# One operand of the half step's VectorE work in PSUM: a graph attention step whose gathers run on GpSimd

## The chip, the cores and the metric

The kernel runs on one core of one Trainium2 chip. The metric is the device time of one execution in microseconds, median over the runs. Times below are microseconds (us) unless marked ns. PE is TensorE, DVE is VectorE, ACT is ScalarE, POOL is GpSimd, SP is SyncE; L770 is line 770 of the kernel before.

## The reference

A block over 4 images of 64 x 64 pixels with 128 channels: an involution (a convolution whose 3 x 3 weights are made from the pixel), added to its input; then a mixture of four experts whose gate is a graph attention over the 16384 tokens and 524288 edges (these name nodes up to 32768; targets past the last token are dropped, sources past it read the last).

```python
def _forward(x, edge_index, W_gat, att_src, att_dst, b_gat, ln_gamma, ln_beta, W1, b1, W2, b2):
    h = (x_flat @ W_gat).reshape(M, HEADS, NUM_EXPERTS)
    src, dst = ...                                   # the edges, and a loop at each node
    a_src = (h * att_src).sum(-1)
    a_dst = (h * att_dst).sum(-1)
    e = leaky_relu(a_src[src] + a_dst[dst], negative_slope=0.2)
    e_max = segment_max(e, dst)
    ee = exp(e - e_max[dst])
    denom = segment_sum(ee, dst)
    alpha = ee / (denom[dst] + 1e-16)
    agg = segment_sum(h[src] * alpha[:, :, None], dst) + b_gat
    scores = layernorm(agg).reshape(M, HEADS, NUM_EXPERTS).mean(1)
    topk_s, topk_i = top_k(scores, 2)
    w = softmax(topk_s)
    for ei in range(NUM_EXPERTS):
        out = out + gate(w, topk_i, ei) * (gelu(x @ W1[ei] + b1[ei]) @ W2[ei] + b2[ei])
x = conv(ln(x)) + x ; x = x + _forward(ln(x), ...)
```

## The kernel before

Each engine has a program of its own, written out in order; semaphores are the only ties between them. First comes the convolution over 32 chunks of four image rows. Then the edges' keys (target node and source node in one integer) are sorted in two lists, by bitonic compares on DVE (`compare`, L1656 to L1663) with transposes on PE and copies back on ACT (`exchange`, `take_exchange`). PE and ACT compute the experts in between, chunk by chunk (`experts`, `expert_copies`): 14 chunks before the first list's exchanges, 10 after them (entry 13 of `EXPERT_CHUNKS`), and the last 8 among the second list's. PE puts four rows of a chunk into PSUM banks 4 to 7, and ACT copies each to `y_new`.

Then the first list's edges are worked through in **half steps** of 64 edges on each of 128 partitions. There are 16 in this run, numbered n = 2k + u here, 0 to 15; step k has halves u = 0 and 1. For each:

- DVE's `new_sources`, two steps ahead, takes the source nodes from the keys.
- POOL's `half` issues one gather for the targets' scores (`adw`, NEAR = 16 neighbouring nodes of 4 heads, L770) and 64 row gathers (`rows_of`, one `indirect_dma_start` of 128 rows each, L770, into `rows_g`, four buffers). At u = 0 it then does `store_fix(k - 3)` (L774) and `fetch_fix(k - 2)`, which carry a node's sums over from one step to the next. POOL's program is in this order and waits where a semaphore isn't there.
- DVE's `half` sorts a part of the second list (`SORTED_BY`), then does `chain_runs(k - 1)` at u = 0 or `mend(k - 2)` at u = 1 (its last line, L2004, lets `store_fix` go), then `edge_scans`. That begins with `nearby`: a one-hot `hot` (L1879) and for each of 4 heads a product (L1884, the pick) and a sum over 16 words (L1886). It then waits for the gathered rows (L1911), makes the scores and running maxima, waits for ACT's exponentials, weights the rows (L1940) and adds up along each partition with a scan (L1948) over 4 heads x 5 parts x 64 edges.
- ACT's `half` takes its exchanges and expert chunks, the small exponentials, and then `edge_exponentials`, whose last copy puts the sums in order for the store to HBM.

After the last half step come a short loop over the second list's edges (`trip`), the gathers of each node's sums (`agg`), the gate, and the mixing of the experts' outputs.

Of the kernel before, what the change touches and what calls it, by code (L numbers as in the profile page):

```python
# [90 lines left out]
def metaformer_block(nc, x, Wr, br, gamma, beta, mean, var, Ws, bs, Wi, bi,  # L91
# [3 lines left out]
    with ctx:  # L95
# [6 lines left out]
        def sem(name):  # L102
# [151 lines left out]
        drop = sb("drop", [P, HEADS, T], F32, edge)  # L254
        keep = sb("keep", [P, HEADS, PARTS - 1, T], F32, edge)
        sums_x = sb("sums_x", [P, HEADS, PARTS - 1, T], F32, edge)
        new = sb("new", [P, HEADS, PARTS - 1, T], F32, edge)
        high = sb("high", [P, 1 + HEADS * T], F32, edge)
# [21 lines left out]

        chain_n = new[0:HEADS].rearrange("p h j t -> p (h j t)")[:, 0:P * (PARTS - 1)].rearrange(
            "p (c j) -> p c j", j=PARTS - 1)
        hot = keep.rearrange("p h j t -> p (h j t)")[:, 0:T * NEAR].rearrange("p (t n) -> p t n", n=NEAR)
        picked = new.rearrange("p h j t -> p (h j t)")[:, 0:T * NEAR].rearrange("p (t n) -> p t n", n=NEAR)
        samples = late[:, 0:P]
# [21 lines left out]
        def sems(names):  # L307
# [33 lines left out]
            sems(f"{n}0 {n}1") for n in ("dch_in", "dch_used", "keys_in", "state_out", "tnT_back", "y_out"))  # L341
        (scored, weighed, state_ready, tails_stored, tails_loaded, chain_scored, chain_weighed,
         summed, chain_ready, chain_stored, cprev_loaded, fix_placed, fix_got, fix_scored,
         fix_weighed, fix_ready, fix_stored, agg_cleared) = sems(
            "scored weighed state_ready tails_stored tails_loaded chain_scored chain_weighed "
            "summed chain_ready chain_stored cprev_loaded fix_placed fix_got fix_scored "
# [554 lines left out]
        def _(pe):  # L901
# [91 lines left out]
            def experts(g, u, turn, q):  # L993
                pe.wait_ge(tnT_back[u], 16 * (turn + 1))
                for e in range(EXPERTS):
                    for a in (0, 1):
                        n = 2 * e + a
                        if some(8 * g + n - 3):
                            pe.wait_ge(hid_ready, 8 * g + n - 3)
                        pe.matmul(bank[n % 4][:, :], w1[:, e, a * P:(a + 1) * P], tnT_in[:, u],  # L1000
                                  start=TR, stop=TR).then_inc(hid_psum, 1)
                pe.wait_ge(hid_ready, 8 * g + 8)
                for r in range(ROWS):
                    if some(g):
                        pe.wait_ge(y_taken, ROWS * (g - 1) + r + 1)
                    po = bank[4 + r]
                    pe.matmul(po[:, :], ones[:, :], b2_rows[:, :], start=TR, stop=FA)
                    for e in range(EXPERTS):
                        for a in (0, 1):
                            last = pe.matmul(po[:, e * C:(e + 1) * C],  # L1010
                                             hid[u][:, 2 * e + a, r * P:(r + 1) * P], w2[:, e, a],
                                             start=FA, stop=e == EXPERTS - 1 and a == 1)
                    last.then_inc(y_psum, 1)
# [21 lines left out]
        def _(act):  # L1035
# [141 lines left out]
            def expert_copies(g, v, turn, q):  # L1177
                for n in range(8):
                    act.wait_ge(hid_psum, 8 * g + n + 1)
                    if n == 0 and some(g - 1):  # L1180
                        act.wait_ge(y_psum, ROWS * (g - 1))
                    act.activation(hid[v][:, n], bank[n % 4][:, :], ACT.Gelu,  # L1182
                                   bias=b1c[:, n // 2, n % 2:n % 2 + 1]).then_inc(hid_ready, 1)

                act.dma_start(tnT_in[:, v], tnT_d[ds(g + 2, 1)].squeeze(0)).then_inc(tnT_back[v], 16)
                if some(turn):
                    act.wait_ge(y_out[v], 32 * turn)
                for r in range(ROWS):
                    act.wait_ge(y_psum, ROWS * g + r + 1)
                    act.activation(y_new[:, v, r], bank[4 + r][:, :], ACT.Copy).then_inc(y_taken, 1)  # L1190
# [8 lines left out]
            def fix_exponentials(k):  # L1199
                act.wait_ge(fix_scored, k + 1)  # L1200
                act.activation(fixe[:, :, :], fixe[:, :, :], ACT.Exp).then_inc(fix_weighed, 1)

            def edge_exponentials(k, u):
                act.wait_ge(scored, 2 * k + u + 1)
                act.activation(keep[:, :, :, :], over(drop[:, :, :], PARTS - 1, 2), ACT.Exp)  # L1205
                if u == 1:
                    act.activation(carry[:, 1], carry[:, 1], ACT.Exp)
                act.activation(new[:, :, 0], score[:, :, :], ACT.Exp).then_inc(weighed, 1)
                act.activation(state_parts[:, u, :, 0], high[:, 1:].rearrange("p (h t) -> p h t", t=T), ACT.Copy)
                act.wait_ge(summed, 2 * k + u + 1)  # L1210
                act.activation(state_parts[:, u, :, 1:], sums_x[:, :, :, :], ACT.Copy).then_inc(state_ready, 1)

# [11 lines left out]
            def half(k, u, j, pair, b):  # L1224
# [49 lines left out]
        def _(dve):  # L1274
# [614 lines left out]
            def edge_scans(k, u, j, pair, b):  # L1889
# [46 lines left out]
                if some(k):  # L1936
                    dve.wait_ge(state_out[u], 16 * k)
                dve.tensor_tensor(drop[:, :, :], drop[:, :, :], reset[:, :, :], ALU.add).then_inc(scored, 1)  # L1938
                dve.wait_ge(weighed, 2 * k + u + 1)
                dve.tensor_tensor(new[:, :, 1:], rows_g[:, w, :, 0:HE].rearrange("p t (h e) -> p h e t", e=EXPERTS),  # L1940
                                  over(new[:, :, 0], EXPERTS, 2), ALU.mult)
                if u == 1:
                    dve.tensor_tensor(carried[:, :, :], sums_x[:, :, :, T - 1], over(carry[:, 1], PARTS - 1, 2),
                                      ALU.mult)
# [244 lines left out]
```

## Time and profile before

| | |
|---|---|
| median of 3 runs | 2920.72 us (2920.6 to 2924.26) |
| span of the profiled execution (its first to its last instruction; it has no other time of its own) | 2918.8 us |
| busy DVE / POOL / PE / ACT | 74% / 45% / 35% / 27% of the span |
| half steps (first L1879 to last L1948) | 1353.9 to 2595.4 us |
| row gathers | 1024, from 1100.0 to 2581.4 us |

The profile is one execution as the hardware recorded it. A row of a timeline has a start, a duration, the engine, the line, what it writes and reads, and in brackets how long the engine stood idle before it and what ended that. "issue" is idle time that no semaphore explains.

### The profile page before, as it was taken

To read this page: it belongs to the slowest core of one execution; us is meant where nothing else is said; L and a number is where in the kernel's file an instruction comes from. 1 tells how busy PE (TensorE), PEld (TensorE's weight loads), DVE (VectorE), ACT (ScalarE), POOL (GpSimd) and SP (SyncE) were. 2 spreads that over 40 slices of the span, in tenths; PEclk is the share of its full clock that TensorE was granted. 3 is DMA by queue.
4 is the path that set the end of the run, shared out by engine and by line. 5 is a ranking of instruction groups with operands and counts; after the bars stand their busy time and mean duration, and the time that the engine had idled before them with its cause. 6 is when DMAs were issued, how large, how long until landed. Compare 5 with 4: busy or idle time off the path is not lost.

```text
span 2918.8 us, 22141 instructions
## 1 busy us (share of the span) xinstructions
PE 1017.2 (35%) x4867; PEld 685.7 (23%) x4867; DVE 2168.2 (74%) x4017; ACT 785.0 (27%) x1576; POOL 1315.3 (45%) x1234
## 2 busy tenths in 40 slices
PE   6777776599811110499333333310000000000000
PEld 3544454366511100266222222210000000000000
DVE  5999989999699974998888898856334313822888
ACT  3555544244411100144322222311000000000344
POOL 0000000000000007777777777778777777835750
PEclk8777666799955555699666666655555555555555
DMA  2222325992100011133231313142212113333676
GB/s 57 72 72 73 78 64 194 384 112 77 71 0 0 0 18 28 30 81 91 44 41 37 42 37 42 37 53 27 19 19 23 19 12 21 46 33 86 182 230 223
DMA packets 259502, 202.29 MB, mean 69 GB/s; under 512 B 101592, under 2 KB 207445, under 8 KB 258902
## 3 DMA queue, kind: packets, MB, share of 16 engines
q1 hardware_dynamic: 189766, 114.21, 17.5%
q0 software_dynamic: 46336, 44.61, 9.1%
q10 hardware_dynamic: 23314, 42.60, 4.6%
q14 instruction: 66, 0.54, 0.1%
q8 instruction: 20, 0.33, 0.0%
HBM read 94.51 MB, written 107.07 MB: 69 GB/s over the span
## 4 chain that ended last, share of the span: by engine, by line
POOL 40%; DVE 15%; issue 15%; PE 14%; DVEq 9%; DMA 3%; ACT 2%; ACTq 0%; POOLq 0%; SPq 0%
POOL sb_rows_g L770 38%; PE bank L1010 4%; DVE sb_xi L1656 3%; PE bank L1000 3%; DVEq L1672 2%; PE bank L926 2%; DVE sb_inv L1361 2%; DVEq L1392 1%; DVE sb_xi L1663 1%; DVEq L1382 1%; DVE sb_y_new L2146 1%; DVE sb_stats L1334 1%; PE bank L917 1%; POOL sb_agg L770 1%; DVEq L1387 1%
## 5 line engine op out<-in xcount | busy, mean ns | idle before, releaser
L770 POOL DMA_INDIRECT sb_rows_g<-scr_node,sb_srcs x1024 | 1107.3, 1081 | 312.1 <-issue 312.1
L1663 DVE TENSOR_TENSOR sb_xi<-sb_xi 128x512 f32<-128x512 f32 (+2 forms) x852 | 427.1, 568 | 46.8 <-ACT sb_xi L1159 33.0
L989 PE MATMUL bank<-sb_ident,sb_xi 128*128 128x128 f32 x448 | 99.5, 410 | 533.6 <-DVE sb_xi L1663 280.1
L770 POOL DMA_INDIRECT sb_hid_y<-scr_level,sb_row_at x8 | 9.3, 1163 | 597.2 <-DVE sb_row_at L1420 595.0
L1656 DVE TENSOR_TENSOR sb_xi<-sb_xi 128x1024 f32<-128x1024 f32 (+2 forms) x258 | 243.5, 944 | 28.2 <-ACT sb_xi L1164 9.5
L1000 PE MATMUL bank<-sb_tnT_in,sb_w 128*128 128x512 f32 x512 | 243.8, 630 | 58.0 <-DVE sb_sinks L1768 33.5
L1010 PE MATMUL bank<-sb_w,sb_hid_y 128*128 128x128 f32 x2048 | 262.6, 282 | 0.0
L1657 DVE TENSOR_TENSOR sb_xi<-sb_xi 128x1024 f32<-128x1024 f32 (+2 forms) x258 | 245.9, 953 | 0.0
L1010 PEld LDWEIGHTS bank<-sb_w,sb_hid_y 128*128 128x128 f32 x2048 | 238.2, 192 | 29.0 <-issue 29.0
L1182 ACT ACTIVATE sb_hid_y<-bank,sb_b1c 128x512 f32<-128x512 f32 x256 | 163.6, 691 | 239.2 <-PE bank L1000 237.5
L765 POOL DMA_DIRECT2D scr_adst_at_starts<-sb_zeros x1 | 1.1, 1057 | 487.3 <-DMA sb_xi<-in_L_ffn_edge_index 487.3
L1031 PE MATMUL bank<-sb_ident,sb_sinks 128*128 128x128 f32 x1 | 0.5, 477 | 616.7 <-DVE sb_sinks L2031 616.7
L989 PEld LDWEIGHTS bank<-sb_ident,sb_xi 128*128 128x128 f32 x448 | 85.7, 216 | 545.5 <-DVE sb_xi L1663 286.2
L1911 DVE TENSOR_TENSOR sb_score<-sb_rows_g,sb_df 128x256 f32<-128x256 f32 x16 | 10.9, 683 | 254.9 <-DMA sb_rows_g<-scr_node,sb_srcs 254.1
L1355 DVE TENSOR_TENSOR sb_prod<-sb_xi,sb_wv 128x1152 f32<-128x1152 f32 x128 | 172.7, 1349 | 23.2 <-ACT sb_xi L1065 18.5
L1205 ACT ACTIVATE sb_keep<-sb_drop 128x1280 f32<-128x1280 f32 x16 | 20.3, 1269 | 614.9 <-DVE sb_drop L1938 614.8
L1361 DVE TENSOR_REDUCE sb_inv<-sb_prod 128x128 f32<-128x1152 f32 x128 | 172.0, 1344 | 5.9 <-issue 1.2
L770 POOL DMA_INDIRECT sb_agg<-scr_state,sb_posi x128 | 132.1, 1032 | 44.2 <-issue 38.7
L1031 PEld LDWEIGHTS bank<-sb_ident,sb_sinks 128*128 128x128 f32 x1 | 0.2, 183 | 616.9 <-DVE sb_sinks L2031 616.9
L1000 PEld LDWEIGHTS bank<-sb_tnT_in,sb_w 128*128 128x128 f32 x512 | 99.7, 202 | 181.4 <-issue 146.0
L1190 ACT ACTIVATE sb_y_new<-bank 128x512 f32<-128x512 f32 x128 | 76.4, 597 | 243.6 <-PE bank L1010 243.6
L926 PE MATMUL bank<-sb_wi,sb_xnT 128*128 128x128 f32 x768 | 140.4, 328 | 0.0
(337 smaller groups left out, 2175.8 us busy)
## 6 DMA issues: line engine op xcount, KB each, us to landing
scr_expert_out<-sb_y_new ACTq DMA_DIRECT2D x64, 512.0 KB, 3.8
sb_y_in<-scr_expert_out SPq DMA_DIRECT2D x32, 1024.0 KB, 6.8
scr_state<-sb_zeros POOLq DMA_DIRECT2D x6, 4096.0 KB, 55.9
sb_rows_g<-scr_node,sb_srcs POOLq DMA_INDIRECT x1024
scr_state<-sb_state SPq DMA_DIRECT2D x16, 768.0 KB, 7.0
scr_tnT<-sb_tnT SPq DMA_DIRECT2D x34, 256.0 KB, 2.0
sb_tnT_in<-scr_tnT ACTq DMA_DIRECT2D x34, 256.0 KB
sb_xa<-in_x SPq DMA_DIRECT2D x64, 128.0 KB, 2.5
```

What stands on the lines that cost most here:

```text
L770: pool.indirect_dma_start(to, None, table, bass.IndirectOffsetOnAxis(ap=index, axis=0), **kw).then_inc(s, 16)
L926: last = pe.matmul(po[:, j * C:(j + 1) * C], xnT[:, u, r, 2 * j:2 * j + P], wi[:, :], start=FA, stop=j == 2)
L989: last = pe.transpose(bank[b][:, m * P:(m + 1) * P], src[:, (4 * b + m) * P:(4 * b + m + 1) * P], ident[:, :])
L1000: pe.matmul(bank[n % 4][:, :], w1[:, e, a * P:(a + 1) * P], tnT_in[:, u], start=TR, stop=TR).then_inc(hid_psum, 1)
L1010: last = pe.matmul(po[:, e * C:(e + 1) * C], hid[u][:, 2 * e + a, r * P:(r + 1) * P], w2[:, e, a], start=FA, stop=e == EXPERTS - 1 and a == 1)
L1182: act.activation(hid[v][:, n], bank[n % 4][:, :], ACT.Gelu, bias=b1c[:, n // 2, n % 2:n % 2 + 1]).then_inc(hid_ready, 1)
L1190: act.activation(y_new[:, v, r], bank[4 + r][:, :], ACT.Copy).then_inc(y_taken, 1)
L1355: return dve.tensor_tensor(to.rearrange("p (g f k) -> p g f k", g=GROUPS, k=KK), patch.rearrange("p (g f k) -> p g f k", g=GROUPS, k=KK), ...
L1361: dve.tensor_reduce(inv[:, r], prod[:, r % 2 * TAPS:(r % 2 + 1) * TAPS].rearrange("p (o k) -> p o k", k=KK), AX.X, ALU.add)
L1656: dve.tensor_tensor(vb[:, :, 0], va[:, :, 0], va[:, :, 1], ALU.min)
L1657: last = dve.tensor_tensor(vb[:, :, 1], va[:, :, 0], va[:, :, 1], ALU.max)
L1663: last = dve.tensor_tensor(vb[:, :, d, :, c], va[:, :, d, :, 0], va[:, :, d, :, 1], ALU.min if c == d else ALU.max)
```

## The change

In `nearby`, in the weighting and in the scan, one of the two operands comes from PSUM bank 7. The experts give that bank up and take banks 4, 5, 6 in turn (`y_bank`, `y_free`). ACT has a new step, `place_around`, ahead of `edge_exponentials`: it copies the target scores (heads first, so that a head's 16 words lie side by side) and the constants 0 to 15 into the bank, and DVE's `nearby` waits for that (`around_placed`). The exponentials of `keep` and of the weights go to the bank too, `keep` once and not five times; a second copy of the weights stays in `new`. `keep`, `sums_x` and `new` have the part ahead of the head, and the scan becomes five, one for each part, over the same `keep`.

```diff
-        hot = keep.rearrange("p h j t -> p (h j t)")[:, 0:T * NEAR].rearrange("p (t n) -> p t n", n=NEAR)
+        flat_keep = bank[7][:, HEADS * T:2 * HEADS * T]
+        weights, keep = (bank[7][:, k * HEADS * T:(k + 1) * HEADS * T].rearrange("p (h t) -> p h t", t=T)
+                         for k in (0, 1))
+        around = bank[7][:, 0:WORDS].rearrange("p (h n) -> p h n", n=NEAR)
+        steps_of = bank[7][:, WORDS:WORDS + NEAR]
...
+        def y_bank(u, r):
+
+            return bank[4 + (r + u) % 3]
+
+        def y_free(g, u, r):
+
+            return ROWS * g + 1 if r == 3 else ROWS * (g - 1) + ((3, 4, 2), (2, 3, 4))[u][r]
...
-                    if some(g):
-                        pe.wait_ge(y_taken, ROWS * (g - 1) + r + 1)
-                    po = bank[4 + r]
+                    if r == 3 or some(g):
+                        pe.wait_ge(y_taken, y_free(g, u, r))
+                    po = y_bank(u, r)
...
+            def place_around(k, u, pair, w):
+                act.wait_ge(adw_in[w], 16 * (pair + 1))
+                if some(2 * k + u):
+                    act.wait_ge(summed, 2 * k + u)
+                act.activation(around, adw[:, w].rearrange("p (n h) -> p h n", h=HEADS), ACT.Copy)
+                act.activation(steps_of, nearest[:, :], ACT.Copy).then_inc(around_placed, 1)
...
-                act.activation(keep[:, :, :, :], over(drop[:, :, :], PARTS - 1, 2), ACT.Exp)
+                act.activation(keep, drop[:, :, :], ACT.Exp)
...
-                act.activation(new[:, :, 0], score[:, :, :], ACT.Exp).then_inc(weighed, 1)
+                act.activation(weights, score[:, :, :], ACT.Exp)
+                act.activation(new[:, 0], score[:, :, :], ACT.Exp).then_inc(weighed, 1)
...
+                place_around(k, u, pair, 2 * b + u)
                 edge_exponentials(k, u)
...
-                dve.tensor_tensor(hot, over(rel[:, w], NEAR, 2), over(nearest[:, :], T), ALU.is_equal)
+                dve.wait_ge(around_placed, 2 * k + u + 1)
+                dve.tensor_tensor(hot[:, :, :], over(rel[:, w], NEAR, 2), over(steps_of, T), ALU.is_equal)
...
-                    dve.tensor_tensor(picked, hot, over(adw[:, w, h:WORDS:HEADS], T), ALU.mult)
+                    dve.tensor_tensor(picked, hot[:, :, :], over(around[:, h], T), ALU.mult)
...
-                dve.tensor_tensor(new[:, :, 1:], rows_g[:, w, :, 0:HE].rearrange("p t (h e) -> p h e t", e=EXPERTS),
-                                  over(new[:, :, 0], EXPERTS, 2), ALU.mult)
+                dve.tensor_tensor(new[:, 1:], rows_g[:, w, :, 0:HE].rearrange("p t (h e) -> p e h t", e=EXPERTS),
+                                  over(weights, EXPERTS, 1), ALU.mult)
...
-                dve.tensor_tensor_scan(flat(sums_x), flat(keep), flat(new), 0.0, ALU.mult, ALU.add).then_inc(summed, 1)
+                for part in range(PARTS - 1):
+                    last = dve.tensor_tensor_scan(flat(sums_x[:, part]), flat_keep, flat(new[:, part]), 0.0,
+                                                  ALU.mult, ALU.add)
+                last.then_inc(summed, 1)
```

How it stands in DVE's order at the start of half step 0's `edge_scans`, before (`sb_keep` holds the one-hot there, `sb_new` the picked words):

```order
L1893 COPY sb_run_now<-sb_run_next 128x3
L1879 TENSOR_TENSOR sb_keep<-sb_rel,sb_nearest 128x1024
L1881 TENSOR_SCALAR sb_afar<-sb_rel 128x64 [waits adw_in0]
L1884 TENSOR_TENSOR sb_new<-sb_keep,sb_adw 128x1024
L1886 TENSOR_REDUCE sb_drop<-sb_new 128x64
```

And in the changed kernel:

```order
L1916 COPY sb_run_now<-sb_run_next 128x3
L1902 TENSOR_TENSOR sb_hot<-sb_rel,bank 128x1024 [waits around_placed]
L1904 TENSOR_SCALAR sb_afar<-sb_rel 128x64 [waits adw_in0]
L1907 TENSOR_TENSOR sb_new<-sb_hot,bank 128x1024
L1909 TENSOR_REDUCE sb_drop<-sb_new 128x64
```

The first product of the half step has a wait for ACT, and `sb_nearest` and `sb_adw` have become the bank; nothing has changed its place. At the half step's end on DVE (weighting, scan, and the first line of `new_sources`), before:

```order
L1938 TENSOR_TENSOR sb_drop<-sb_drop,sb_reset 128x256
L1940 TENSOR_TENSOR sb_new<-sb_rows_g,sb_new 128x4x256 [waits weighed]
L1948 SCALAR_TENSOR_TENSOR sb_sums_x<-sb_keep,sb_new 128x1280
L1519 TENSOR_SCALAR sb_srcs<-sb_keyb 128x64 [waits keys_in0]
L1520 TENSOR_SCALAR sb_clsi<-sb_keyb 128x65
```

And in the changed kernel:

```order
L1961 TENSOR_TENSOR sb_drop<-sb_drop,sb_reset 128x256
L1963 TENSOR_TENSOR sb_new<-sb_rows_g,bank 128x1024 [waits weighed]
L1972 SCALAR_TENSOR_TENSOR sb_sums_x<-bank,sb_new 128x256 x5
L1541 TENSOR_SCALAR sb_srcs<-sb_keyb 128x64 [waits keys_in0]
L1542 TENSOR_SCALAR sb_clsi<-sb_keyb 128x65
```

One scan of 1280 elements (the order prints a scan by this name) has become five of 256. On ACT, from the end of the ten expert chunks into half step 0, before:

```order
L1193 DMA scr_expert_out<-sb_y_new 64x4x512
L477 REGISTER_ALU
L477 COMPARE_AND_BRANCH
L1205 ACT_TABLE_LOAD [waits scored]
L1205 ACTIVATE sb_keep<-sb_drop 128x1280 [waits counted]
L1208 ACTIVATE sb_new<-sb_score 128x4x64
```

And in the changed kernel:

```order
L1205 DMA scr_expert_out<-sb_y_new 64x4x512
L489 REGISTER_ALU
L489 COMPARE_AND_BRANCH
L1219 ACTIVATE bank<-sb_adw 128x64 [waits adw_in0,counted]
L1220 ACTIVATE bank<-sb_nearest 128x16
L1224 ACT_TABLE_LOAD
L1224 ACTIVATE bank<-sb_drop 128x256 [waits scored]
L1227 ACTIVATE bank<-sb_score 128x256
L1228 ACTIVATE sb_new<-sb_score 128x256
```

The two copies into the bank stand behind all expert chunks and ahead of the half step's exponentials.

## Rows read from the trace of the kernel before

**Rows 1.** The page: the chain that ended last, by line.

```profile
POOL sb_rows_g L770 38%; PE bank L1010 4%; DVE sb_xi L1656 3%; PE bank L1000 3%; DVEq L1672 2%; PE bank L926 2%; DVE sb_inv L1361 2%; DVEq L1392 1%; DVE sb_xi L1663 1%; DVEq L1382 1%; DVE sb_y_new L2146 1%; DVE sb_stats L1334 1%; PE bank L917 1%; POOL sb_agg L770 1%; DVEq L1387 1%
```

**Rows 2.** The page's costliest groups: busy, mean ns | idle before, its releaser.

```profile
L770 POOL DMA_INDIRECT sb_rows_g<-scr_node,sb_srcs x1024 | 1107.3, 1081 | 312.1 <-issue 312.1
...
L1911 DVE TENSOR_TENSOR sb_score<-sb_rows_g,sb_df 128x256 f32<-128x256 f32 x16 | 10.9, 683 | 254.9 <-DMA sb_rows_g<-scr_node,sb_srcs 254.1
```

**Rows 3.** One line's instructions, L770: count, ns min/median/max, first and last start.

```profile
L770 POOL DMA_INDIRECT sb_rows_g<-scr_node,sb_srcs x1024: 940/944/3073, 1100.0 to 2581.4; - x171
```

**Rows 4.** Timeline of POOL in half step 1: start, duration, engine, line, operands.

```profile
1424.25 0.94 POOL L770 DMA_INDIRECT sb_rows_g<-scr_node,sb_srcs  x1 [0.30 <-issue]
...
1433.22 1.74 POOL L770 DMA_INDIRECT sb_rows_g<-scr_node,sb_srcs  x1 [0.30 <-issue]
1435.27 0.94 POOL L770 DMA_INDIRECT sb_rows_g<-scr_node,sb_srcs  x1 [0.30 <-issue]
1436.52 1.79 POOL L770 DMA_INDIRECT sb_rows_g<-scr_node,sb_srcs  x1 [0.30 <-issue]
...
1455.52 1.99 POOL L770 DMA_INDIRECT sb_rows_g<-scr_node,sb_srcs  x1 [0.30 <-issue]
1457.82 2.96 POOL L770 DMA_INDIRECT sb_rows_g<-scr_node,sb_srcs  x1 [0.31 <-issue]
```

**Rows 5.** Timeline of DVE in the same stretch.

```profile
1424.23 1.28 DVE L1657 TENSOR_TENSOR sb_xi<-sb_xi 128x1024 f32<-128x1024 f32 x1
...
1432.17 1.97 DVE L1884 TENSOR_TENSOR sb_new<-sb_keep,sb_adw 128x1024 f32<-128x1024 f32 x1
1434.21 1.22 DVE L1886 TENSOR_REDUCE sb_drop<-sb_new 128x64 f32<-128x1024 f32 x1
...
1446.75 0.69 DVE L1904 TENSOR_TENSOR_SCAN sb_df<-sb_same,sb_dch_h 128x256 f32<-128x256 f32 x1
...
1448.01 0.43 DVE L1908 TENSOR_TENSOR sb_df<-sb_df,sb_drop 128x256 f32<-128x256 f32 x1
1448.51 0.68 DVE L1911 TENSOR_TENSOR sb_score<-sb_rows_g,sb_df 128x256 f32<-128x256 f32 x1
...
1454.48 2.28 DVE L1940 TENSOR_TENSOR sb_new<-sb_rows_g,sb_new 128x1024 f32<-128x1024 f32 x1 [1.74 <-ACT sb_new L1208]
...
1457.19 2.82 DVE L1948 TENSOR_TENSOR_SCAN sb_sums_x<-sb_keep,sb_new 128x1280 f32<-128x1280 f32 x1
```

**Rows 6.** Timeline of DVE and ACT around half step 0.

```profile
1353.87 1.22 DVE L1879 TENSOR_TENSOR sb_keep<-sb_rel,sb_nearest 128x1024 f32<-128x1024 f32 x1
...
1387.72 2.29 DVE L1940 TENSOR_TENSOR sb_new<-sb_rows_g,sb_new 128x1024 f32<-128x1024 f32 x1 [12.52 <-ACT sb_new L1208]
...
1382.38 0.60 ACT L1190 ACTIVATE sb_y_new<-bank 128x512 f32<-128x512 f32 x1 [1.70 <-PE bank L1010]
1383.18 1.41 ACTq L1193 DMA_DIRECT2D scr_expert_out<-sb_y_new  x2
...
1386.11 1.27 ACT L1205 ACTIVATE sb_keep<-sb_drop 128x1280 f32<-128x1280 f32 x1
1387.29 0.40 ACT L1208 ACTIVATE sb_new<-sb_score 128x256 f32<-128x256 f32 x1
```

**Rows 7.** Timeline of DVE and POOL in half steps 5 and 7.

```profile
1732.99 0.19 DVE L2004 TENSOR_TENSOR sb_fixo<-sb_cprev,sb_fixs 128x20 f32<-128x20 f32 x1
...
1734.22 1.18 POOL L774 DMA_INDIRECT scr_state<-sb_fixo,sb_fixo_i  x1 [0.30 <-issue]
...
1911.76 0.18 DVE L2002 TENSOR_TENSOR sb_cprev<-sb_cprev,sb_fixe 128x20 f32<-128x20 f32 x1 [12.86 <-ACT sb_fixe L1201]
...
1912.10 0.18 DVE L2004 TENSOR_TENSOR sb_fixo<-sb_cprev,sb_fixs 128x20 f32<-128x20 f32 x1
...
1923.56 1.02 POOL L774 DMA_INDIRECT scr_state<-sb_fixo,sb_fixo_i  x1 [0.30 <-issue]
```

**Rows 8.** Windows, tile `rows_g`: from and to, length, busy us (count), PE clock, DMA.

```profile
1923.50:2583.00 659.50, 23.72 (x16) 486.41 (x448) 0.50 0.24 25
```

More of the change, by code:

```diff
@@ L185, in metaformer_block @@
         carry = sb("carry", [P, 3, HEADS])
-        carried = sb("carried", [P, HEADS, PARTS - 1])
+        carried = sb("carried", [P, PARTS - 1, HEADS])
         keyb = sb("keyb", [P, 2, 1 + 2 * T], I32)
@@ L254, in metaformer_block @@
         drop = sb("drop", [P, HEADS, T], F32, edge)
-        keep = sb("keep", [P, HEADS, PARTS - 1, T], F32, edge)
-        sums_x = sb("sums_x", [P, HEADS, PARTS - 1, T], F32, edge)
-        new = sb("new", [P, HEADS, PARTS - 1, T], F32, edge)
+        hot = sb("hot", [P, T, NEAR], F32, edge)
+        sums_x = sb("sums_x", [P, PARTS - 1, HEADS, T], F32, edge)
+        new = sb("new", [P, PARTS - 1, HEADS, T], F32, edge)
         high = sb("high", [P, 1 + HEADS * T], F32, edge)
@@ L279, in metaformer_block @@
         edge.close()
-        chain_n = new[0:HEADS].rearrange("p h j t -> p (h j t)")[:, 0:P * (PARTS - 1)].rearrange(
+        chain_n = new[0:HEADS].rearrange("p j h t -> p (j h t)")[:, 0:P * (PARTS - 1)].rearrange(
             "p (c j) -> p c j", j=PARTS - 1)
-        hot = keep.rearrange("p h j t -> p (h j t)")[:, 0:T * NEAR].rearrange("p (t n) -> p t n", n=NEAR)
-        picked = new.rearrange("p h j t -> p (h j t)")[:, 0:T * NEAR].rearrange("p (t n) -> p t n", n=NEAR)
+        flat_keep = bank[7][:, HEADS * T:2 * HEADS * T]
[3 more added lines that the diff above has]
+        steps_of = bank[7][:, WORDS:WORDS + NEAR]
+        picked = new.rearrange("p j h t -> p (j h t)")[:, 0:T * NEAR].rearrange("p (t n) -> p t n", n=NEAR)
         samples = late[:, 0:P]
@@ L341, in metaformer_block @@
             sems(f"{n}0 {n}1") for n in ("dch_in", "dch_used", "keys_in", "state_out", "tnT_back", "y_out"))
-        (scored, weighed, state_ready, tails_stored, tails_loaded, chain_scored, chain_weighed,
+        (around_placed, scored, weighed, state_ready, tails_stored, tails_loaded, chain_scored, chain_weighed,
          summed, chain_ready, chain_stored, cprev_loaded, fix_placed, fix_got, fix_scored,
          fix_weighed, fix_ready, fix_stored, agg_cleared) = sems(
-            "scored weighed state_ready tails_stored tails_loaded chain_scored chain_weighed "
+            "around_placed scored weighed state_ready tails_stored tails_loaded chain_scored chain_weighed "
             "summed chain_ready chain_stored cprev_loaded fix_placed fix_got fix_scored "
@@ L1189, in expert_copies @@
                     act.wait_ge(y_psum, ROWS * g + r + 1)
-                    act.activation(y_new[:, v, r], bank[4 + r][:, :], ACT.Copy).then_inc(y_taken, 1)
+                    act.activation(y_new[:, v, r], y_bank(v, r)[:, :], ACT.Copy).then_inc(y_taken, 1)
                 act.wait_ge(y_taken, ROWS * (g + 1))
@@ L1201, in fix_exponentials @@
                 act.activation(fixe[:, :, :], fixe[:, :, :], ACT.Exp).then_inc(fix_weighed, 1)
+            def place_around(k, u, pair, w):
[4 more added lines that the diff above has]
+                act.activation(steps_of, nearest[:, :], ACT.Copy).then_inc(around_placed, 1)
             def edge_exponentials(k, u):
                 act.wait_ge(scored, 2 * k + u + 1)
-                act.activation(keep[:, :, :, :], over(drop[:, :, :], PARTS - 1, 2), ACT.Exp)
+                act.activation(keep, drop[:, :, :], ACT.Exp)
                 if u == 1:
                     act.activation(carry[:, 1], carry[:, 1], ACT.Exp)
-                act.activation(new[:, :, 0], score[:, :, :], ACT.Exp).then_inc(weighed, 1)
+                act.activation(weights, score[:, :, :], ACT.Exp)
+                act.activation(new[:, 0], score[:, :, :], ACT.Exp).then_inc(weighed, 1)
                 act.activation(state_parts[:, u, :, 0], high[:, 1:].rearrange("p (h t) -> p h t", t=T), ACT.Copy)
                 act.wait_ge(summed, 2 * k + u + 1)
-                act.activation(state_parts[:, u, :, 1:], sums_x[:, :, :, :], ACT.Copy).then_inc(state_ready, 1)
+                act.activation(state_parts[:, u, :, 1:], sums_x.rearrange("p j h t -> p h j t"),
+                               ACT.Copy).then_inc(state_ready, 1)
             def exchanges(first, end):
@@ L1939, in edge_scans @@
                 dve.wait_ge(weighed, 2 * k + u + 1)
-                dve.tensor_tensor(new[:, :, 1:], rows_g[:, w, :, 0:HE].rearrange("p t (h e) -> p h e t", e=EXPERTS),
-                                  over(new[:, :, 0], EXPERTS, 2), ALU.mult)
+                dve.tensor_tensor(new[:, 1:], rows_g[:, w, :, 0:HE].rearrange("p t (h e) -> p e h t", e=EXPERTS),
+                                  over(weights, EXPERTS, 1), ALU.mult)
                 if u == 1:
-                    dve.tensor_tensor(carried[:, :, :], sums_x[:, :, :, T - 1], over(carry[:, 1], PARTS - 1, 2),
+                    dve.tensor_tensor(carried[:, :, :], sums_x[:, :, :, T - 1], over(carry[:, 1], PARTS - 1, 1),
                                       ALU.mult)
```

## The prediction

> **What bounds the kernel now.** VectorE (DVE) is the busiest engine, but a busy share says nothing of who sets the end, so I first read the chain that ended last [rows 1]. Its largest entry is line 770 on GpSimd (POOL): the row gathers, 38%. So in the stage of the half steps, 1350 to 2590 us, I asked who waits for whom [rows 2]. DVE's line 1911, which needs the 64 gathered rows of its half step, sat idle 254 us before 7 of its 16 executions; the 1024 gathers sat idle 312 us, all of it their own 0.30 us between two. POOL never waits for DVE there; DVE, when it is ahead, waits for POOL. The end is set by how long 1024 gathers take.
>
> Then I asked how long one takes. The undisturbed gather is 0.94 us (least 940, median 944 ns), but the longest took 3073 ns and the mean is 1081 [rows 2, 3]. The timelines of POOL and of DVE over one half step, laid side by side, say where the rest comes from [rows 4, 5]. The gather that starts at 1433.22 takes 1.74; DVE's pick product (line 1884) runs from 1432.17 to 1434.14, and the gather ends 0.82 us after that. The gather that begins at 1435.27, under the reduction of line 1886, takes 0.94. The gather at 1455.52 ends 0.7 to 0.8 us after line 1940, and that at 1457.82 takes 2.96 and ends 0.8 us after the scan of line 1948. So a gather that begins under one of these three lines stands still until that DVE instruction is over. All three read two tensors from SBUF; the reduction, which reads one, does no harm. One row speaks less clearly: the sort's compare at 1424.23 reads two as well, and the gather at 1424.25 takes 0.94. That gather begins within 0.02 us of the compare's start, so it may have read before the compare did.
>
> **What the stretch is worth.** The two picks shown cost 1.74 and 1.79 less 0.94 each, 0.8 on the mean, so the four of a half step 3.3 us of POOL's time; the other two lines cost 1.99 + 2.96 less 1.88 = 3.07 us. That is 6.4 us, or 102 us over 16 half steps. In every one of the changed instructions one of the two tensors now lies in PSUM. No row shows a DVE instruction with one operand in each memory; between a stretch that stays whole and none at all I take none, since the form is nearest to the reduction, with one SBUF input. The other two-input lines are left as they are.
>
> The Trainium skill (SBUF — State Buffer, Who interferes with whom) says two things here: VectorE with two SBUF inputs contends with a GpSimd instruction that reads SBUF, and with one it does not; but also that a probe saw `tensor_tensor` leave descriptor generation alone. Rows 4 and 5 speak against the second; if it held, the stretch would have another cause and could stay, as in the second rival below.
>
> **What the change does to DVE.** POOL's gain is worth something only where DVE does not stop POOL, so DVE's time comes next. Per half step:
> - Picks: the picked words were read 4 words apart (`adw[:, w, h:WORDS:HEADS]`); they now lie side by side. Lines 1879 and 1884 have the same size, 1024 elements, and take 1.22 and 1.97 [rows 5, 6]; the words' stride is what differs. That a stride costs is seen again at 256 elements: line 1911, which reads rows 20 words apart, takes 0.68, line 1908 takes 0.43 [rows 5]. Bounds for the new pick: 1.22 and 1.97. I take 1.22, so 4 x 0.75 = 3.0 us less.
> - Exponentials: ACT's 1.27 us over 1280 elements and 0.40 over 256 become three of 256, 1.20 in all: 0.5 us less in the wait before line 1940 [rows 6].
> - Scans: one of 2.82 becomes five of 256. A scan of 256 takes 0.69, so the five lie between 2.82 and 3.46: I take 0.5 more.
> - Line 1940 keeps its strided rows: 0.
>
> Together 3.0 us less per half step. Neither half of this reaches the end by itself, since DVE waits for the gathers later; at the very end, after the last gather, 0.5 less and 0.5 more cancel.
>
> The Trainium skill (VectorE: DVE Perf Modes, The TRN2 errata) gives a source in PSUM 120 fixed cycles against 58 for SBUF. For 11 instructions that would be an estimated 0.7 us per half step, and would put the end some 5 us later than my sum; no row here has this form.
>
> **What it adds: a wait at half step 0.** DVE may now start `nearby` only when ACT has copied `adw` into the bank, and ACT does that behind all it has queued. In half step 0 ACT is still copying the ten expert chunks out of PSUM: its last copy starts at 1382.38, two DMA issues end at 1384.6, and two copies smaller than those of 0.40 us follow, so the bank is ready near 1385.3. Before, DVE started line 1879 at 1353.87 and met ACT only at line 1940, where it waited 12.52 us [rows 6]. So DVE starts 31.4 us later; the wait of 12.52 shrinks to the ordinary 1.74 (half step 1) less 0.5, which is 11.3 less; picks 3.0 less; scans 0.5 more: half step 0 ends 17.6 us later. In later half steps ACT is done with its experts before DVE needs the bank, and the two copies are hidden; the closest is half step 7, where DVE waits 12.86 us for ACT anyway just ahead of line 2004 [rows 7] and the copies come right behind that; the later DMA wait for `adw` on ACT holds nothing that DVE lacks.
>
> **Where DVE then stops POOL.** POOL's `store_fix` (line 774) in half step 6 needs DVE's `mend` (line 2004), which ends 1733.18; POOL starts it at 1734.22: a cover of 1.0 us. In half step 8 it is 1912.28 against 1923.56, a cover of 11.3 [rows 7]. DVE reaches the first 17.6 - 4 x 3.0 = 5.6 us later, so POOL starts it at 1739.8, though its own gathers would have let it come at 1734.2 - 5 x 6.4 = 1702. The gain of the first five half steps turns into a wait of 38 us. From there to the second point POOL took 189.3 us; without the stretches of half steps 5, 6 and the picks of 7 (2 x 6.4 + 3.3 = 16.1) it takes 173.2: 1913.0. DVE's own time there is 1912.28 + 17.6 - 6 x 3.0 = 1911.9, and POOL follows 1.0 later: 1912.9, just under that. Before: 1923.56. Gain so far: 10.6 us.
>
> After that point DVE is ahead of POOL (the seven waits of line 1911 all lie there), and POOL sets the end alone. What its gathers lose: by the pattern 3.07 (half step 7) + 7 x 6.4 + 3.3 (half step 15) = 51 us; by the window from 1923.5 to 2583, 486.41 - 448 x 0.944 = 63.5 us of stretch of every cause [rows 8]. I take 57, half way. Sum: 10.6 + 57 = 68 us. The rest, from the last gather on, moves along unchanged. So do the experts: with three banks in turn, a chunk's fourth row waits for the copy of its first, 0.60 us long, and PE takes 2.3 us for each row between (ACT waits 1.70 for it before each copy) [rows 6].
>
> The profiled span is 2918.8, the median of the runs 2920.7, 1.9 us more around it: 2920.7 - 68 = **2853 us**.
>
> **The rivals.**
> - Picks stay at 1.97 (PSUM read no faster). Then DVE gains nothing per half step and half step 0 ends 20.6 later; POOL passes the second point at 1933.9, 10.3 late, and gains 57 after it: 47 less, 2874. For it: no row has the form. Against: the stride is gone in either memory.
> - The stretch isn't tied to the second SBUF input, but to the length of a DVE instruction of this kind. The picks, shorter by 0.74, would stretch 0.1 each instead of 0.8, the other two lines as before: 2.9 of 6.4 goes. After the second point 57 x 2.9 / 6.4 = 26 us are gained, and 1913.0 moves to 1739.8 + 189.3 - 16.1 x 2.9 / 6.4 = 1921.8, 2 us gained: 2893. For it: the stretches grow with the instruction's length. Against: the reduction is 1.22 long and harmless. The gather beside the sort's compare speaks for it too.
> - The late start doesn't reach POOL, and all 102 us count: 2819. Against it: a cover of 1.0 us at half step 6.
> - Slower: reading PSUM beside SBUF is slow on DVE. DVE would hold POOL at half step 8. The sum is zero when DVE is 67 us late there (57 + 10.3); 20.6 is the wait of half step 0, so 47 us over 7 half steps, 6.7 each: picks of 1.97 + 1.7 = 3.7 us. At 4.3 us a pick it would be 9.3 more per half step, and 2939.
>
> **How the numbers follow.** The forecast (2843 to 2866 with its own bounds: 51 to 63.5 of stretch, scans 2.82 to 3.46, 0.1 us more for a pick) 0.64; picks not faster 0.13; stretch tied to length 0.10; all 102 us 0.05; slow PSUM, slower 0.04; and 0.04 for a gain that something unseen takes back to nothing. A measurement of this kernel tells about 0.2% from no change. So faster 0.92, same 0.04, slower 0.04. The range, 2838 to 2896, takes in the first three cases and leaves 0.13 outside.
>
> **What would show it.** In the changed trace: gathers under lines 1907, 1963 and 1972 at 0.94; picks at 1.2 to 1.3 us; a DVE wait of about 31 us for ACT line 1220 in half step 0; a POOL wait of some 38 us at line 774 of half step 6, for DVE's `mend`, and next to none in half step 8; the last gather near 2514 instead of 2581. If gathers still take 1.8 us beside the picks, the reading of rows 4 and 5 was wrong; if picks stay near 2 us, that of the stride; if POOL doesn't wait at half step 6, my time for DVE.

## The result, and the profile after

The changed kernel took 2840.61 us (median of 4, 2834.66 to 2846.96) against 2920.66 us for the kernel before (median of 4, 2912.6 to 2924.26): ratio 0.9721, interval 0.9689 to 0.9754, 80 us less. The forecast was 2853, 12 us above.

The page of the changed kernel: its span, the chain that ended last, and the groups that answer to [rows 1, 2].

```profile
span 2832.8 us, 22266 instructions
...
DVE 28%; PE 21%; POOL 18%; DVEq 14%; issue 10%; ACT 5%; DMA 3%; ACTq 1%; SPq 0%; POOLq 0%
...
L782 POOL DMA_INDIRECT sb_rows_g<-scr_node,sb_srcs x1024 | 1001.4, 978 | 312.1 <-issue 311.7
...
L1934 DVE TENSOR_TENSOR sb_score<-sb_rows_g,sb_df 128x256 f32<-128x256 f32 x16 | 10.9, 682 | 210.8 <-DMA sb_rows_g<-scr_node,sb_srcs 210.0
```

The mean gather fell from 1081 to 978 ns; the pause of 0.30 us between two is as it was. The row gathers were 38% of the chain [rows 1]; on this page they are 16% (all of POOL 18%), and DVE is 28%. The timeline of POOL under the picks, the weighting and the scans of half step 1 answers to [rows 4]:

```profile
1438.79 0.94 POOL L782 DMA_INDIRECT sb_rows_g<-scr_node,sb_srcs  x1 [0.31 <-issue]
1440.04 0.94 POOL L782 DMA_INDIRECT sb_rows_g<-scr_node,sb_srcs  x1 [0.30 <-issue]
1441.29 0.94 POOL L782 DMA_INDIRECT sb_rows_g<-scr_node,sb_srcs  x1 [0.30 <-issue]
...
1452.68 1.22 POOL L782 DMA_INDIRECT sb_rows_g<-scr_node,sb_srcs  x1 [0.30 <-issue]
...
1459.20 0.94 POOL L782 DMA_INDIRECT sb_rows_g<-scr_node,sb_srcs  x1 [0.30 <-issue]
1460.45 0.94 POOL L782 DMA_INDIRECT sb_rows_g<-scr_node,sb_srcs  x1 [0.30 <-issue]
1461.69 0.94 POOL L782 DMA_INDIRECT sb_rows_g<-scr_node,sb_srcs  x1 [0.30 <-issue]
```

And DVE's in the same stretch, which answers to [rows 5]:

```profile
1438.98 1.22 DVE L1907 TENSOR_TENSOR sb_new<-sb_hot,bank 128x1024 f32<-128x1024 f32 x1
1440.27 1.22 DVE L1909 TENSOR_REDUCE sb_drop<-sb_new 128x64 f32<-128x1024 f32 x1
...
1452.46 0.68 DVE L1934 TENSOR_TENSOR sb_score<-sb_rows_g,sb_df 128x256 f32<-128x256 f32 x1
...
1457.92 2.29 DVE L1963 TENSOR_TENSOR sb_new<-sb_rows_g,bank 128x1024 f32<-128x1024 f32 x1 [1.19 <-ACT sb_new L1228]
...
1460.64 3.01 DVE L1972 TENSOR_TENSOR_SCAN sb_sums_x<-bank,sb_new 128x256 f32<-128x256 f32 x5
```

Gathers that begin well inside the picks, the weighting or the scans now take 0.94: the one at 1459.20 begins 1.28 us into the weighting and ends before it. Beside a product that still reads two tensors from SBUF (L1934 at 1452.46) one of 1.22 is left.

For the whole program I put what each of the 1024 row gathers took above 0.944 us down to the DVE line that it overlapped longest (the sums are mine, over the rows of each trace; the last two columns are experiments told of below):

| stretch of row gathers under, us | before | changed | everything in SBUF | words alone in PSUM |
|---|---|---|---|---|
| one-hot, picks and their reductions | 59.4 | 0.2 | 17.0 | 0.2 |
| weighting | 17.5 | 0.0 | 15.3 | 14.5 |
| scans | 26.1 | 0.0 | 3.9 | 3.9 |
| all other lines | 37.7 | 34.6 | 34.5 | 32.7 |

Under the changed lines the gathers lost 103 us before and lose 0.2 now; the prediction counted 102. Not all of that reaches the end. The timelines around half step 0, then of POOL in half steps 6 and 8, answer to [rows 6, 7]:

```profile
1374.42 0.28 ACT L1219 ACTIVATE bank<-sb_adw 128x64 f32<-128x64 f32 x1 [1.85 <-issue]
1374.64 0.17 ACT L1220 ACTIVATE bank<-sb_nearest 128x16 f32<-128x16 f32 x1
...
1344.59 0.17 DVE L1916 COPY sb_run_now<-sb_run_next 128x3 f32<-128x3 f32 x1
1374.84 1.22 DVE L1902 TENSOR_TENSOR sb_hot<-sb_rel,bank 128x1024 f32<-128x1024 f32 x1 [30.08 <-ACT bank L1220]
...
1726.05 0.18 DVE L2030 TENSOR_TENSOR sb_fixo<-sb_cprev,sb_fixs 128x20 f32<-128x20 f32 x1
1727.11 1.02 POOL L786 DMA_INDIRECT scr_state<-sb_fixo,sb_fixo_i  x1 [40.59 <-DVE sb_fixo L2030]
...
1896.44 0.18 DVE L2030 TENSOR_TENSOR sb_fixo<-sb_cprev,sb_fixs 128x20 f32<-128x20 f32 x1
1899.38 1.02 POOL L786 DMA_INDIRECT scr_state<-sb_fixo,sb_fixo_i  x1 [0.30 <-issue]
```

DVE waits 30 us for two small copies that stand behind ACT's ten expert chunks. Some 350 us after that, POOL has stood still for 40.6 us before `store_fix` of half step 6, waiting for DVE's `mend`. In half step 8 it comes 2.8 us after `mend` and doesn't wait.

The two profiled executions differ by 86.0 us of span: 9.2 ahead of half step 0, 72.7 from there to the last row gather, and 4.1 behind it. So stage times below are counted from half step 0, from DVE's copy to `run_now` (at 1353.8 before, 1344.6 here), to the end: 1565.0 us before, and 1488.2 and 1489.4 in two profiles of the changed kernel.

### The profile page after: what moved, and what is told of

It is laid out like the page before. It is cut to its first block, busy times and chain, and to the rows that moved or that the text cites. A ratio compares the mean times of both kernels' runs of the same rounds, so it can differ in the third digit from the quotient of the medians.

```text
span 2832.8 us, 22266 instructions
## 1 busy us (share of the span) xinstructions
PE 1002.3 (35%) x4867; PEld 675.7 (24%) x4867; DVE 2124.0 (75%) x4081; ACT 780.2 (28%) x1624; POOL 1202.6 (42%) x1234
## 4 chain that ended last, share of the span: by engine, by line
DVE 28%; PE 21%; POOL 18%; DVEq 14%; issue 10%; ACT 5%; DMA 3%; ACTq 1%; SPq 0%; POOLq 0%
POOL sb_rows_g L782 16%; PE bank L1022 7%; DVE sb_xi L1678 7%; PE bank L1012 6%; DVEq L1694 5%; DVE sb_xi L1685 3%; DVE sb_inv L1383 2%; PE bank L938 2%; DVE sb_hid_y L1518 2%; DVEq L1414 2%; PE bank L1001 2%; DVEq L1404 2%; DVE sb_y_new L2172 1%; PE bank L1019 1%; DVE sb_new L1907 1%
## 5 line engine op out<-in xcount | busy, mean ns | idle before, releaser
L782 POOL DMA_INDIRECT sb_rows_g<-scr_node,sb_srcs x1024 | 1001.4, 978 | 312.1 <-issue 311.7
L1012 PE MATMUL bank<-sb_tnT_in,sb_w 128*128 128x512 f32 x512 | 238.5, 618 | 57.7 <-DVE sb_sinks L1790 33.5
L1377 DVE TENSOR_TENSOR sb_prod<-sb_xi,sb_wv 128x1152 f32<-128x1152 f32 x128 | 172.7, 1350 | 20.0 <-ACT sb_xi L1077 15.3
L1934 DVE TENSOR_TENSOR sb_score<-sb_rows_g,sb_df 128x256 f32<-128x256 f32 x16 | 10.9, 682 | 210.8 <-DMA sb_rows_g<-scr_node,sb_srcs 210.0
L1224 ACT ACTIVATE bank<-sb_drop 128x256 f32<-128x256 f32 x16 | 6.2, 388 | 538.6 <-DVE sb_drop L1961 538.6
```

The costliest lines, as they stand in the source:

```text
L782: pool.indirect_dma_start(to, None, table, bass.IndirectOffsetOnAxis(ap=index, axis=0), **kw).then_inc(s, 16)
L1377: return dve.tensor_tensor(to.rearrange("p (g f k) -> p g f k", g=GROUPS, k=KK), patch.rearrange("p (g f k) -> p g f k", g=GROUPS, k=KK), ...
```

## The experiments

Two theories stood against each other. **A**: a gather that begins under a DVE instruction with two SBUF inputs stands still until that ends; one operand in PSUM sets it free. **B**: the stretch belongs to long instructions of this kind, and it went because picks and scans became short. With either, the late start at half step 0 may or may not pass to POOL.

**Everything in SBUF.** The changed kernel with its layout and order, but what lay in the bank lies in a tile in SBUF.

```diff
+        half_work = sb("half_work", [P, 2 * HEADS * T], F32, edge)
...
-        flat_keep = bank[7][:, HEADS * T:2 * HEADS * T]
+        flat_keep = half_work[:, HEADS * T:2 * HEADS * T]
...
-        around = bank[7][:, 0:WORDS].rearrange("p (h n) -> p h n", n=NEAR)
+        around = half_work[:, 0:WORDS].rearrange("p (h n) -> p h n", n=NEAR)
```

> The changed kernel with its four tiles (words, constants, weights, keep) in SBUF instead of the bank: the new layout, the five scans and ACT's step stay, only PSUM goes. Theory A (a gather that begins under a DVE instruction with two SBUF inputs stands still until that instruction ends): picks are 1.22 us and side by side now, so a gather falls into step with them and loses about 0.1 us per pick; it loses about 1.05 us under the weighting (2.28 us) and some 1 us under the five scans: 2.4 us per half step, 19 us after the second point where DVE can hold POOL and a few before it, so 20 to 24 us more than the changed kernel, about 2862 us. Theory B (only the length of a DVE instruction counts, wherever its operands lie): nothing changes, 2841 us, within 5.

Measured: 2863.02 us against 2922.32 for the kernel before on the same chip (0.9787, 0.9729 to 0.9845); from half step 0 to the end 24.8 us more than the changed kernel, as A has it. Its gathers on the page, 35 ns longer than in the changed kernel:

```profile
L783 POOL DMA_INDIRECT sb_rows_g<-scr_node,sb_srcs x1024 | 1037.3, 1013 | 312.0 <-issue 311.7
```

POOL and DVE on the timeline of its half step 1:

```profile
1442.45 0.94 POOL L783 DMA_INDIRECT sb_rows_g<-scr_node,sb_srcs  x1 [0.30 <-issue]
1443.69 1.05 POOL L783 DMA_INDIRECT sb_rows_g<-scr_node,sb_srcs  x1 [0.30 <-issue]
...
1459.29 2.68 POOL L783 DMA_INDIRECT sb_rows_g<-scr_node,sb_srcs  x1 [0.30 <-issue]
1462.27 1.40 POOL L783 DMA_INDIRECT sb_rows_g<-scr_node,sb_srcs  x1 [0.30 <-issue]
...
1442.70 1.23 DVE L1908 TENSOR_TENSOR sb_new<-sb_hot,sb_half_work 128x1024 f32<-128x1024 f32 x1
1445.29 1.23 DVE L1908 TENSOR_TENSOR sb_new<-sb_hot,sb_half_work 128x1024 f32<-128x1024 f32 x1
...
1458.93 2.29 DVE L1964 TENSOR_TENSOR sb_new<-sb_rows_g,sb_half_work 128x1024 f32<-128x1024 f32 x1 [1.19 <-ACT sb_new L1229]
...
1461.64 3.05 DVE L1973 TENSOR_TENSOR_SCAN sb_sums_x<-sb_half_work,sb_new 128x256 f32<-128x256 f32 x5
```

The weighting is the clean pair: 2.29 us long in both kernels. With one input in the bank, the gather at 1459.20 took 0.94; with both in SBUF, that at 1459.29 takes 2.68 and ends 0.75 us after the weighting; the next, under the scans, takes 1.40. So with all of them: 14 gathers that begin more than 0.1 us into the weighting take 1.75 to 2.69 here and end 0.75 to 0.76 us after it, and 19 such gathers of the changed kernel take 0.94 to 0.95. Only the memory of one operand differs, so B falls as the whole cause, and A is shown.

The picks show something else. With their words side by side they stretch a gather by no more than 0.1 us even from SBUF (1443.69). The gather at 1442.45 began 0.25 us ahead of a pick and ran through it at 0.94, so one that is under way isn't stopped; the next begins near the pick's end. A pick and its reduction take 2.59 us (1442.70 to 1445.29), and two gathers with their pauses 0.94 + 0.30 + 1.05 + 0.30 = 2.59: the gathers have fallen in step with DVE. In the table above, the layout alone takes 42 of the picks' 59 us and 22 of the scans' 26, in all 67 of the 103; the bank takes the other 36.

**Words alone in PSUM.** The picks' operands stay in the bank; `weights` and `keep` go to SBUF.

```diff
...
-        weights, keep = (bank[7][:, k * HEADS * T:(k + 1) * HEADS * T].rearrange("p (h t) -> p h t", t=T)
+        weights, keep = (half_work[:, k * HEADS * T:(k + 1) * HEADS * T].rearrange("p (h t) -> p h t", t=T)
```

> Half of the change: words and constants in the bank, weights and keep in SBUF. Theory A: the picks leave the gathers alone (0.94), the weighting with two SBUF inputs costs the gather under it about 1.05 us again, and the five scans (0.66 us each, end to end) about 1 us together: 2 us per half step, 16 us after the second point, so 2857 us. Theory B: 2841 us.

Measured: 2855.04 us (0.9744, 0.9686 to 0.9803, against the same runs of before), 11.1 us more than the changed kernel from half step 0 on. That is 5 less than A's figure, since five short scans stretch the gathers by 0.24 us per half step (3.9 / 16), not by 1. The weighting's 0.9 (14.5 / 16) is as expected, and the picks' column is clean again. The same instruction does harm or not, by where its second input lies.

**Words 4 apart in the bank.** Only the order of the copied words changes.

```diff
-        around = bank[7][:, 0:WORDS].rearrange("p (h n) -> p h n", n=NEAR)
+        around = bank[7][:, 0:WORDS].rearrange("p (n h) -> p h n", h=HEADS)
```

> The changed kernel, but the words stay in their old order in the bank, so that a pick reads them 4 apart from PSUM. Theory A: the gathers beside the picks stay at 0.94 us however long a pick is. If the stride costs in PSUM what it did in SBUF (1.97 us a pick), DVE is 3.0 us later per half step and holds POOL at half step 8 some 16 us longer: 2857 us; if it costs nothing there, 2841. Theory B: with picks of 1.97 us the gathers under them go back to 1.74 to 1.80, 3.3 us per half step, 27 us after the second point and the 16 before it: about 2884 us.

The lines of the picks, one source line each: of this kernel, of the changed one, and of the one with everything in SBUF (least, median and greatest ns):

```profile
L1907 DVE TENSOR_TENSOR sb_new<-sb_hot,bank x64: 1220/1221/1223, 1399.9 to 2500.4; 128x1024 f32<-128x1024 f32 x64
```

```profile
L1907 DVE TENSOR_TENSOR sb_new<-sb_hot,bank x64: 1220/1221/1223, 1376.2 to 2476.9; 128x1024 f32<-128x1024 f32 x64
```

```profile
L1908 DVE TENSOR_TENSOR sb_new<-sb_hot,sb_half_work x64: 1224/1225/1226, 1377.2 to 2500.3; 128x1024 f32<-128x1024 f32 x64
```

The stride that made 1.97 us of 1.22 in SBUF costs nothing in the bank. So this run gave no slow pick, and could not set A apart from B as it was meant to: 2838.14 us (0.9687, 0.9631 to 0.9744), 0.6 us from the changed kernel in the stage.

**The wait alone.** The kernel before, and in it only the wait: ACT copies the words to a tile `aside` in SBUF that nobody reads, and `nearby` waits for it.

```diff
+                act.activation(aside[:, 0:WORDS], adw[:, w], ACT.Copy)
+                act.activation(aside[:, WORDS:], nearest[:, :], ACT.Copy).then_inc(around_placed, 1)
...
+                dve.wait_ge(around_placed, 2 * k + u + 1)
                 dve.tensor_tensor(hot, over(rel[:, w], NEAR, 2), over(nearest[:, :], T), ALU.is_equal)
```

> The kernel before, with the new wait alone: ACT copies the words and constants to a tile in SBUF that nobody reads, and DVE's nearby waits for that; the operands stay where they were. My theory: DVE starts half step 0 31 us later and ends it 20 us later, POOL's cover of 1.0 us at half step 6 is gone and it waits about 19 us there, and since nothing became faster all of it stays: about 1584 us from half step 0 to the end against 1565, and some 19 us slower than before. Rival (the late start is absorbed by DVE's slack): the time of before.

Measured: 2936.11 us against 2919.06 (1.0057, 1.0033 to 1.0081), 17 us more, and 17.3 more from half step 0 on. The timeline of POOL in half step 6:

```profile
1759.47 1.33 POOL L775 DMA_INDIRECT scr_state<-sb_fixo,sb_fixo_i  x1 [21.14 <-DVE sb_fixo L2012]
```

The late start passes to POOL almost whole: `mend` comes 18.8 us later than before, against a cover of 1.0.

**Words placed early.** ACT makes half step 0's two copies ahead of the ten expert chunks. This kernel was run twice, the second time beside the changed kernel as it is.

```diff
                         act.wait_ge(search_over, 1)
+                        place_around(0, 0, 0, 0)
                     over_experts(act, expert_copies, n)
...
-                place_around(k, u, pair, 2 * b + u)
+                if some(2 * k + u):
+                    place_around(k, u, pair, 2 * b + u)
```

> The changed kernel with ACT's copy of half step 0's words put ahead of the ten expert chunks, so that the wait at half step 0 goes (30.1 us in the profile of the changed kernel), but the old wait for the exponentials (12.5 us before) comes back. My theory: DVE ends half step 0 about 16 us earlier, reaches the two places where it holds POOL 16 us earlier, POOL's wait at half step 6 shrinks from 40.6 to about 25 us, and all of it reaches the end: 2825 us. Rival: POOL, not DVE, sets the second point by its own pace from somewhere else, or the late start is absorbed: 2841 us.

> The kernel with half step 0's words copied early, once more. In its profile the stretch from half step 0 to the end was 20 us shorter than in the changed kernel, and POOL's wait at half step 6 was 21 us and not 41, as my theory has it; but its times were those of the changed kernel, with a convolution of 540 us in the profiled run. If that was the draw of the convolution: some 15 to 20 us below the changed kernel's times on this chip. If early words cost the same 20 us somewhere ahead of half step 0: no difference again, and a long convolution in the profile again.

> The changed kernel once more, beside the others on one chip. The convolution ahead of the half steps took between 513 and 540 us in the profiles so far, with PE's granted clock going up and down between its two levels in another pattern each time, so a single time says little within 10 us. From the start of half step 0 to the end the profiles should agree: 1488 us here as in the first profile of the changed kernel, whatever the convolution took.

Measured: 2838.57 us the first time (0.9697 of before, 0.9636 to 0.9758) and 2825.79 the second (0.9676, 0.9644 to 0.9707), beside 2838.81 for the changed kernel (0.9741, 0.9702 to 0.9781). The first time shows no gain over the changed kernel and misses the 2825 that was expected; the second shows 13 us. The stage says it plainly both times: 20 us less from half step 0 to the end than the changed kernel (1468.1 and 1469.8 against 1488.2 and 1489.4), and POOL in half step 6 waits half as long; the timeline of the second:

```profile
1729.45 1.02 POOL L786 DMA_INDIRECT scr_state<-sb_fixo,sb_fixo_i  x1 [19.96 <-DVE sb_fixo L2032]
```

What hid this the first time lies ahead of half step 0, which began at 1371.2 us in its profile and at 1344.6 in the changed kernel's. That is no price of the early words: the kernel with words 4 apart, which has none, began it at 1367.9. It is the convolution: from its last reciprocal (L1367 in the changed kernel) to half step 0 all ten profiles take 829.0 to 830.3 us.

**POOL's step moved behind.** Words placed early, and in steps 3 to 5 `store_fix` and `fetch_fix` come at u = 1 and not at u = 0, so that POOL has issued one more half step of gathers before it needs `mend`.

```diff
-                if u == 0 and (not isinstance(k, int) or k > 2):
-                    store_fix(k - 3)
+                tail_or_first = (isinstance(j, int) and j < 0) or (isinstance(k, int) and k == 2)
+                if u == (0 if tail_or_first else 1):
+                    if not isinstance(k, int) or k > 2:
+                        store_fix(k - 3)
...
```

> Early words, and POOL's store_fix and fetch_fix of steps 3 to 5 one half step later in its order (behind the gathers of half u = 1), so that DVE's mend is long over when POOL comes to them. My theory, that these two waits are where DVE still holds POOL: POOL waits nowhere between half step 0 and the last gather, the last 21 us of waiting go, and from half step 0 to the end it takes about 1447 us (1468 with early words alone, 1488 changed, 1565 before). Rival: DVE holds POOL elsewhere, or the later fetch stops DVE's mend so that gathers wait for sources: no gain over early words alone.

Measured: 2809.72 us (2801.68 to 2829.8) against 2919.06 for before (0.9636, 0.9594 to 0.9678) and 2838.81 for the changed kernel; it beats both. From half step 0 to the end 1451.7 us, 36.5 less than the changed kernel and 16 to 18 less than with early words alone, where 1447 was expected. From half step 0 to the last row gather POOL waits for no other engine for longer than its usual 0.3 us. POOL's waits by what it waited for (total, times, longest), of the changed kernel and of this one:

```profile
POOL scr_state L786 <- DVE sb_fixo L2030: 50.5, 2, 40.6
```

```profile
POOL scr_state L786 <- DVE sb_fixo L2034: 10.0, 1, 10.0
```

The wait of 40.6 is gone; that of 10, behind the last row gather, was there before (9.9).

## Why the prediction was right

**The stretch.** It goes whole, as taken: 103 us of it lay under the changed lines, 102 were counted, and 0.2 is left. The sum agrees better than its terms: picks with their one-hot had 59 where 53 were counted, weighting and scans 44 where 49 were. And the prediction put all of it down to PSUM, while 67 of the 103 go by the new layout alone, with everything in SBUF; the step from two SBUF inputs to one is worth the other 36, and 24.8 us of the stage.

That the stretch hangs on the second SBUF input, and not on length, rested in the prediction on one reduction, and its row can't carry that. The gather of 1435.27 begins 0.16 us before that reduction's end (1435.43), and with the 0.75 to 0.8 us that a stopped gather takes after the end it would have had about 0.94 either way. So this step was right by luck as far as the row goes. The weighting at one length with its operand in either memory shows it, and the changed kernel has gathers that begin early in a reduction and take 0.94 (23 that begin more than 0.4 us before its end take 0.94 to 0.95):

```profile
1385.54 0.94 POOL L782 DMA_INDIRECT sb_rows_g<-scr_node,sb_srcs  x1 [0.30 <-issue]
...
1385.30 1.22 DVE L1909 TENSOR_REDUCE sb_drop<-sb_new 128x64 f32<-128x1024 f32 x1
```

The row that spoke less clearly, the gather of 0.94 beside the sort's compare, is a near thing and no exception. Before the change 66 gathers begin within 0.05 us behind a compare of L1657. Of these 63 take 0.94, and the compare then takes 1.27 to 1.29; three take 2.0, and the compare 1.22, as here:

```profile
1643.79 1.22 DVE L1657 TENSOR_TENSOR sb_xi<-sb_xi 128x1024 f32<-128x1024 f32 x1
...
1643.82 2.00 POOL L770 DMA_INDIRECT sb_rows_g<-scr_node,sb_srcs  x1 [0.30 <-issue]
```

That fits the prediction's guess, that one of the two may read first; a gather that begins 0.25 us ahead isn't stopped (1442.45 with everything in SBUF).

The Trainium skill (SBUF — State Buffer, Who interferes with whom) has VectorE contend with GpSimd's reads when both its inputs come from SBUF, and not with one; the weighting agrees, 2.68 against 0.94 us. The probe that the Trainium skill reports there, in which `tensor_tensor` did not stall a DMA, isn't borne out by these gathers (2.68 us); they also read their indices from SBUF (`sb_srcs`), and which part of a gather stands still no run shows.

**DVE.** Picks 1.22 as taken. The five scans 3.01 us where 3.3 was taken (between 2.82 and 3.46), so DVE gains a little more than 3.0 per half step: from the end of half step 0 (the last line of `new_sources`) to the `mend` of half step 5 it takes 325.0 us after 338.4, 13.4 less where 12.0 was predicted. The weighting kept its 2.28, and the wait before it fell to 1.19 (1.24 predicted).

The Trainium skill (VectorE: DVE Perf Modes, The TRN2 errata) would add an estimated 0.7 us per half step for sources in PSUM; these rows don't show it: the pick takes 1.221 us from the bank and 1.225 from SBUF, the weighting 2.28 from either.

**The wait at half step 0** was 30.1 us (31.4 predicted), and half step 0 ended 15.6 us later (17.6).

**Where DVE stops POOL.** 40.6 us at half step 6 (38 predicted), none at half step 8, where POOL came by its own pace, as predicted. The gain at that point was 15.0 us, not 10.6: DVE's `mend` came only 2.2 us later than before (5.6 predicted), and POOL took 172.3 us from there (173.2 predicted). After it POOL gained 57.7, 57 predicted, which is in part luck: 57 was the middle of 51 and 63.5. The window of the row gathers, which answers to [rows 8]:

```profile
1899.20:2501.00 601.80, 23.71 (x16) 432.93 (x448) 0.50 0.26 27
```

It was 486.41 before, so the row gathers gained 53.5; the other 4.3 came from POOL's 25 other transfers there (all of POOL was busy 515.6 us in that window before and 457.8 now), which the sum left out. Of the row gathers' stretch 432.93 - 448 x 0.944 = 10 us are left.

**The difference of 12 us.** 2840.6 lies 2 us below the forecast's own bounds and inside the range. The medians differ by 80. The sum was 68; the terms above make 72.7 of it in the profiled execution, mostly since the gain at half step 8 was 4.4 larger. The work behind the last gather took 4.1 less, where 0 was taken (336.5 us before, 334.3 with the wait alone, 330.8 to 333.0 in all kernels with the new layout, so up to 2 of it may be the spread between executions). That makes 77; what is left of the 80 can't be told from the stage ahead of half step 0, which varies by more than that.

**The rivals.** Picks that stay slow: 1.22. A stretch tied to length alone: falls with everything in SBUF, where the weighting, as long as before, keeps 15.3 of its 17.5 us; but the short picks and scans lose much of theirs there, as this rival had it for the picks. All 102 us: the wait of 40.6 takes a part of them back, and the last experiment shows how much. A slow PSUM on DVE: no row has it.

## What to carry to other kernels

Before you count a gain on the engine that sets the end, look for the places where another engine can stop it: here a wait of 30 us for two small copies behind long work cost 20 us at the end, and moving two steps on top of the change gave another 29 us, 2809.7 against 2838.8. A gather that began under a DVE instruction with two SBUF inputs lost most of that instruction's length here (2.0 us beside a scan of 2.82), so split long ones or put one operand in PSUM; and test the layout apart from the memory, since the new layout alone gave 52 of the 77 us from half step 0 on. Compare such edits stage by stage from a common instruction, where an earlier stage varies by more than they are worth.

## What was not expected of the hardware

- Words 4 apart cost a DVE product 0.75 us of 1.97 from SBUF, and nothing from PSUM (1.221 us either way).
- Gathers fall in step with a repeated pair of DVE instructions of nearly their own period (2.59 us for both), and then lose 0.1 us to each, not 0.8.
- The convolution has the same work in all ten profiles, but half step 0 began between 1344.6 and 1371.2 us, and all but about 1 us of that lies in the convolution. DVE's wait there for ACT's square root goes the same way. Its line in the changed kernel, and with words placed early the first time:

```profile
L1367 DVE RECIPROCAL sb_rstd<-sb_sd 128x4 f32<-128x4 f32 x64 | 11.0, 172 | 15.3 <-ACT sb_sd L1091 13.9 <-ACT sb_sd L1059 1.5
```

```profile
L1369 DVE RECIPROCAL sb_rstd<-sb_sd 128x4 f32<-128x4 f32 x64 | 11.1, 173 | 38.7 <-ACT sb_sd L1091 35.7 <-ACT sb_sd L1059 3.0
```

PE's mean granted clock over the first 256 us was 0.74 and 0.73 of full speed, and so doesn't tell the two apart; what sets the length of that stage stays open.
